# Logic attention: half a set of scores in each of eight convolution steps, turned scores copied two units later, chain product ahead of the convolution

## The reference, cut to what matters

```python
S1 = einsum('bhnd,bhmd->bhnm', q1, k1) * scale;  S2 = the same of q2, k2
A1, A2 = softmax(S1), softmax(S2)
Cr = log(A1 @ A2 + eps);  Cl = log(A2 @ A1 + eps)
feat = stack([S1, S2, S1^T, S2^T, Cr, Cl])             # 6 channels
hid = gelu(conv1 (16 x 6) of feat + b1)                # point by point over n, m
gates = sigmoid(conv2 (4 x 16) of hid + b2)
Smix = S1 + g_and*S2 + g_or*(logaddexp(S1, S2) - S1) - g_not*(0.5*S2) + g_chain*Cr
y = softmax(Smix) @ v1 + w * A1 @ (A2 @ v2)            # the second term is the chain product
```

## Time and profile before

| | us |
|---|---|
| median of 3 runs | 2436.7 |
| the profiled execution's own time | 2430.69 |
| its span | 2428.9 |
| TensorE matmul busy | 2174.1 (90%) |
| VectorE busy | 1793.3 (74%) |
| ScalarE busy | 1708.1 (70%) |
| GpSimd busy | 586.3 (24%) |

### The profile page before, as it was taken

One profiled execution on the slowest core, in us unless ns is written; L12 is line 12 of the kernel. 1 busy time (PEld: TensorE's weight loads), 2 busy tenths in 40 slices (PEclk: granted clock), 3 DMA queues, 4 the chain that ended last, 5 costly groups with the idle time before them and its releaser, 6 DMA issues. The chain is left out here.

```text
span 2428.9 us, 55288 instructions
## 1 busy us (share of the span) xinstructions
PE 2174.1 (90%) x22198; PEld 1519.2 (63%) x22198; DVE 1793.3 (74%) x2576; ACT 1708.1 (70%) x3089; POOL 586.3 (24%) x262
## 2 busy tenths in 40 slices
PE   6689999999999999998746979988599999999998
PEld 3554444444444444443235859865499999999998
DVE  4348999899998998988656344544688888888887
ACT  3478888888888888888742245751677777777776
POOL 0234545454544544444200011430000000000000
PEclk9589999999999999999857977999599999999999
DMA  6287777787787777787510000000321221222220
GB/s 177 74 236 215 217 202 225 214 229 199 219 228 219 214 213 218 218 225 206 121 56 1 2 9 2 2 23 19 121 70 62 73 74 66 73 74 74 74 74 20
DMA packets 113320, 305.66 MB, mean 126 GB/s; under 512 B 20479, under 2 KB 57465, under 8 KB 112554
## 3 DMA queue, kind: packets, MB, share of 16 engines
q1 hardware_dynamic: 113066, 302.13, 43.1%
HBM read 169.11 MB, written 80.65 MB: 103 GB/s over the span
## 5 line engine op out<-in xcount | busy, mean ns | idle before, releaser
L750 ACT ACTIVATE la_hid<-ps,la_b 128x904 f32<-128x904 f32 (+1 forms) x480 | 451.1, 989 | 115.5 <-PE ps L602 114.5
L1721 PE MATMUL ps<-ls_xm,ls_w_in_parts 128*128 128x226 f16 x3072 | 468.3, 262 | 12.1 <-DVE ls_xm L1802 8.6
L1729 PE MATMUL ps<-ls_state_parts,ls_w_rec_parts 128*128 128x226 f16 x2976 | 447.9, 259 | 0.0
L1748 ACT ACTIVATE ls_gates<-ps,ls_bias 128x226 f32<-128x226 f32 x768 | 301.6, 446 | 126.9 <-PE ps L1729 126.8
L602 PE MATMUL ps<-la_pairs,la_w 32*64 32x452 f32 x3584 | 332.9, 592 | 26.4 <-ACT la_hid L750 23.2
L1721 PEld LDWEIGHTS ps<-ls_xm,ls_w_in_parts 128*128 128x128 f16 x3072 | 295.3, 97 | 21.7 <-issue 8.9
L1729 PEld LDWEIGHTS ps<-ls_state_parts,ls_w_rec_parts 128*128 128x128 f16 x2976 | 285.2, 96 | 6.3
L615 PE MATMUL ps<-la_hid,la_w 128*32 128x452 f32 x1856 | 251.8, 579 | 1.0 <-ACT la_opened L756 1.0
L576 POOL TENSOR_TENSOR la_P<-la_S,la_top 113x904 f32<-113x904 f32 x64 | 153.4, 2397 | 266.5 <-DVE la_top L863 266.5
L602 PEld LDWEIGHTS ps<-la_pairs,la_w 32*64 32x64 f32 x3584 | 78.3, 134 | 196.2 <-issue 113.4
L564 POOL TENSOR_TENSOR la_P<-la_P,la_inv 113x904 f32<-113x904 f32 x64 | 153.6, 2420 | 192.7 <-DVE la_inv L842 192.7
(11 more groups left out here) (292 smaller groups left out, 4336.1 us busy)
## 6 DMA issues: line engine op xcount, KB each, us to landing
la_pairs<-la_maps SPq DMA_DIRECT2D x224, 452.0 KB, 6.1
la_gate<-la_opened SPq DMA_DIRECT2D x448, 113.0 KB, 3.5
ls_w_all<-ls_weights SPq DMA_DIRECT2D x32, 904.0 KB, 4.1
la_maps<-la_ST SPq DMA_DIRECT2D x32, 791.0 KB
la_maps<-la_S SPq DMA_DIRECT2D x32, 791.0 KB
ls_m_all<-ls_masks SPq DMA_DIRECT2D x32, 456.0 KB, 3.6
la_maps<-la_Cr SPq DMA_DIRECT2D x32, 395.5 KB
la_maps<-la_Cl SPq DMA_DIRECT2D x32, 395.5 KB
```

Of the source, the lines that this page charges most:

```text
L750: act.activation(hid[:, u % 4, 0:n], ps[:, bank:bank + n, 0:HALF], ACT.Gelu_apprx_tanh, bias=b1[:])\
L1721: mm = pe.matmul(out_j, w_in_parts[:, w, e, j, :], xm[:, t % 2, e, :, x, 0:N], start=((w, x) == PASSES[0]), stop=(t == 0 and (w, x) == PAS ...
L1729: mm = pe.matmul(out_j, w_rec_parts[:, w, e, j, :], state_parts[:, x, e], start=False, stop=((w, x) == PASSES[-1]))
L1748: return act.activation(dst, ps[:, n % 3 * 2 + j // 2, j % 2 * 256:j % 2 * 256 + C], ACT.Tanh if j == 3 else ACT.Sigmoid, bias=bias[:, e, ...
```

## The change

On TensorE, each of the eight steps makes half a set of scores, so that set 0 is complete after step 1, set 1 after step 3, set 2 after step 5 and set 3 after step 7. In step 0 the chain product stands ahead of the convolution. On ScalarE the two copies of turned scores stand after units 3 and 7 (before: after units 1 and 5). Nothing else differs: the waits of each helper, the DMAs and VectorE's and GpSimd's lists are the same.

```diff
-    SCORED = (0, 2, 4, 6)
...
                     for g in range(STEPS):
+                        if g == 0 and ok(p + 1):
+                            chain(p + 1)
                         if ok(p):
                             conv(p, g)
-                        if g == 0 and ok(p + 1):
-                            chain(p + 1)
                         if ok(p) and g:
                             gates(p, g - 1)
-                        if ok(p + 3) and g in SCORED:
-                            score(p + 3, SCORED.index(g), 0)
-                            score(p + 3, SCORED.index(g), 1)
+                        if ok(p + 3):
+                            score(p + 3, g // 2, g % 2)
...
-                        if ok(z) and u in (1, 5):
-                            turned_scores(z, u // 5)
+                        if ok(z) and u in (3, 7):
+                            turned_scores(z, u // 4)
```

## The result

The changed kernel takes 2446.75 us (median of 6 runs, 2441.78 to 2452.75) against 2437.93 of the kernel before: ratio 1.0051, 95% interval 1.0036 to 1.0066. It is slower; the forecast was 2412, range 2401 to 2432. The chance of slower stood at 0.10.

The account below looks back on a forecast made before the run. Bound: a loop of waits, pair 3's opening released by TensorE or DMA landings. 29 periods of 33.20 us (962.8) plus 2 falls of 1.8 make 966.4, 24.5 less: 2436.7 to 2412.2; range 2401 to 2432.

Parts of the forecast that it names:

- The clock: TensorE, step 0: splitting the 2.76 us stretch without convolution leaves 2 falls in place of 8, each costing 1.8 us.
- My first rival: Falls of the clock stay at about 8, as a 1 us pause remains; 13.7 us less, 2423; chance 0.25.
- The rival on the other side: Each added stay among scores' tiles costs TensorE extra, or 16 or more periods have falls; slower, up to 2469; chance 0.10.
- Half sets: TensorE's eight steps: a half takes at most 0.65 us, so pair 3 could open at 21.84, gaining 0.84.
- the rival of dear entries: TensorE's four added entries per period cost extra; at 0.65 us each, 32 us more, 2469; chance of slower 0.10.
- The copies of turned scores: ScalarE, behind units 3 and 7: it waits 0.5 us or less; no cost beyond what the steps hold.
- Chain product first: Start of step 0: VectorE starts its next list without a gap, 0.39 us earlier.
- What ends last: Opening of pair 3: DMA landings move 0.39 us earlier, those openings to 22.62; mean 22.36, period 33.20.
- the next limits: Behind the DMA landings: TensorE at 21.84, and GpSimd's second subtraction, which allows a gain of up to 0.85 us.
- Straight scores: VectorE, set 2 complete at 15.40 us after the period's zero: it waits almost nothing.
- The sum: Periods 0 to 28: 962.8 us plus two falls of 1.8 make 966.4 against 990.9, 24.5 less.

Follow-up runs that it names:

- after_fill: The changed kernel with 6 unread matmuls behind the half set of step 0 from period 3 on; 2391.12 us, ratio 0.9824 to the kernel before.
- fill_narrow: The changed kernel with the narrow matmuls of step 0's first half set issued twice from period 3 on; 2422.65 us, ratio 0.9945 to the kernel before.
- fill_two: The changed kernel with 2 unread wide matmuls in the pause of step 0; 2399.17 us, ratio 0.9846 to the kernel before.
- chain_only: The kernel before with only the chain product moved ahead of convolution step 0, scores in whole sets; 2426.84 us, ratio 0.9974 to the kernel before.
- set0_whole: The changed kernel with set 0 whole in step 0, no scores in step 1, sets 1 to 3 in halves; 2402.95 us, ratio 0.9873 to before.

## Why the prediction was wrong, step by step

**The clock: this step failed.** I wrote "I take it that most go, and put 2 in place of 8", because the convolution now split the stretch of 2.76 us. There were 20. The split shortened the stretch ahead of the zero but made a new one behind it: half a set is taken out of the 1.3 us that a whole one fills, and 1.0 to 1.2 us of nothing stay until ScalarE has freed the banks. I had that pause in my own numbers ("1 us until the first unit is out") and judged the new stretch by its length beside 2.76, having looked only at what preceded the falls of the kernel before. The length was right (516.24 to 518.09 is 1.85, where I had 1.8); that a shorter one is safe was the error. after_fill shows it: with this pause filled, one fall is left from period 3 on, where there were 18. My first rival named the pause too, but with 8 falls. A fall also costs 3.0 where I had 1.8: one of 7 us costs 2.7 (35.31 - 32.58), and 6 of the falls last 10 us or more. That the steps with half a set each leave TensorE less slack would explain the 2.7; no run tests it. Together 60.4 instead of 3.6, 57 too little. The rival on the other side named this as a second way ("if the clock falls in 16 or more of 29 periods"), and 20 is past that point.

**Half sets: right.** Pair 3 was to be ready for TensorE at 21.84; it opens at 505.94 - 484.34 = 21.60. Eight stays among the scores' tiles cost nothing that shows, so the rival of dear entries is out. By the rule of the Trainium skill, "TensorEngine Tiling (Array Packing)", Key Properties, each of them drains TensorE; the 21.60 leaves no room for a price beside the matmuls' own time. The copies of turned scores are right too: ScalarE waits 0.36 us before that of set 0 in this period, within the 0.5 that I allowed.

**Chain product first: right, and mis-sized.** VectorE has no gap: L845 follows L953. It starts 1.49 ahead of the zero, 0.66 earlier than in the earlier trace rows and not 0.39: the two instructions overlap by 0.1, and VectorE's tail stands 0.15 earlier, since ScalarE's tail is about that much longer: from the opening to L775 it takes 4.21 us, against 4.01 in the earlier trace rows, as L775 now waits for GpSimd. SP's pair 0 goes out at 494.83, 10.49 after the zero, where I had 10.7.

**What ends last: right in kind.** The landings moved with L877's end, and further than it: pair 0 goes out 0.65 earlier, and the openings that the DMA releases come at a mean of 21.97 in the changed kernel and 22.11 in after_fill, where I had 22.62 (23.01 before). Why they gained the rest is not shown. With the clock held the DMA releases pair 3 in 22 of the 26 clean periods of after_fill. Where it doesn't, the next limits are TensorE at 21.60 and GpSimd, as named: its subtraction ends at 510.11 and L775 starts at 510.15, which is 25.81 (I had "not before 25.9"). Clean periods came out at 32.69 and 32.85 (after_fill) instead of 33.20; over 29 periods that is 10 to 15 us that I gave away.

**Straight scores: nearly.** VectorE waits 0.7 us for set 2 in the clean period shown, not "almost nothing", and 3.41 after a fall.

**The sum:** 966.4 forecast, 1008.3 measured: 56.8 from the clock, -14.8 from the clean periods. after_fill, where the clock stays up as I had assumed, has 955.0 and a median of 2391.

## What to carry to other kernels

When work is spread out to fill an engine's steps, look at the place that it was taken from: here the whole set was what covered TensorE while it waited for ScalarE, and 0.6 us taken away there cost more in clock (45 us) than the 28 us of better steps brought. In a kernel whose clock already falls now and then, count the falls in the trace before and after as a term of their own, and hold the clock by some filling before judging the rest. Two waits that end within tenths of each other have to be moved together: with the clock held, one part alone gave 3.5 us, the other 10.8, and both 22.4. And a test that is meant to hold one thing equal has to be read in all its periods: one of fill_narrow's shows a pause of 0.68, nearly fill_two's, and most of them 0.79.

## What the runs showed of the hardware

A pause of 1.0 to 1.2 us on TensorE per period of 33 us, with half a set of scores ahead of it, went with the clock at its lower level for 160 of 1008 us. I had not expected so short a pause to do that, with the engine's row busy for 94% of a clean period (30.62 of 32.58). The Trainium skill, "TensorE: Matmul & The Clock Gate", section "A second HAM failure mode: psum-queue depth-cycling", says that short idles between groups of matmuls can make the clock go back and forth; this trace agrees. It does so in 20 of 29 periods. Filling the pause held the clock: five kernels with it closed have none or one fall in periods 3 to 28, and so has fill_two, which still has 0.40 to 0.56 us of it. With mostly 0.77 to 0.80 us left, 21 of the 26 periods have a fall, whether one wide matmul (128 rows) or four narrow ones (32 rows) had filled the rest. The length of that pause is not all: 0.33 us in chain_only and 0.33 to 0.49 in set0_whole still go with 14 and 15 short falls, and which periods have one follows a pattern (every second in chain_only from period 8 on). Why, these runs don't settle.
